# Windowed attention in six layers: each head's scores and values on its own 64 rows of TensorE, and a new split of the PSUM banks

## What is computed

```python
def attn_layer(x, Wqkv, qs, ksc, Wo):          # 16 heads of 64
    q, k, v = jnp.split(x @ Wqkv, 3, -1)
    q = l2norm(q) * qs; k = l2norm(k) * ksc
    q, k = rotary(q), rotary(k)
    out = local_attention(q, k, v)             # windows of 32 queries, 64 keys
    return out @ Wo

def local_attention(q, k, v):                  # this window and the one before it
    sim = jnp.einsum('bhwie,bhwje->bhwij', bq, bk2) * QK_SCALE
    sim = jnp.where(mask, -jnp.finfo(sim.dtype).max, sim)
    attn = jax.nn.softmax(sim, -1)
    return jnp.einsum('bhwij,bhwje->bhwie', attn, bv2)

def ffn_layer(x, ...):                         # layer norm, then a gated MLP
    a, gate = jnp.split(hg, 2, -1)
    return a * jax.nn.gelu(gate, approximate=False) @ W2 + b2
```

## Time and profile before

| what | value |
| --- | --- |
| three runs | 4799.48, 4806.38, 4807.76 us; median 4806.38 |
| profiled execution, own time | 4815.81 us |
| its span, first to last instruction | 4814.0 us |
| TensorE matmul busy, share of the span | 93% |
| VectorE busy | 78% |
| ScalarE busy | 63% |
| GpSimd busy | 37% |
| granted TensorE clock, mean | 0.964 |

### The profile page before, as it was taken

The page is one execution under the profiler, slowest core; times in us unless marked ns, Lnnn a source line. Parts: engine busy times, 40 slices in busy tenths (PEclk is TensorE's granted clock), DMA queues, the critical chain, the costliest instruction groups (busy, mean ns, idle before and its releaser), DMA issues. The chain is left out here.

```text
span 4814.0 us, 118285 instructions
## 1 busy us (share of the span) xinstructions
PE 4463.8 (93%) x45408; PEld 3472.9 (72%) x45408; DVE 3737.9 (78%) x6437; ACT 3030.9 (63%) x4718; POOL 1797.1 (37%) x966
## 2 busy tenths in 40 slices
PE   7999589999999999999999999999999999689999
PEld 2333278787787877778778777787778788468878
DVE  6888588888888888888888888888888888556554
ACT  5777357676766766676667666676766676334333
POOL 0000155554454544555445554455545555000000
PEclk9988799999999999999999999999999999889999
DMA  0000122222322222222222222222222222100000
GB/s 28 5 5 5 46 58 60 54 55 51 84 51 58 58 57 70 58 56 54 70 63 56 54 59 69 58 58 58 51 74 60 58 55 55 61 7 5 9 7 5
DMA packets 132797, 229.65 MB, mean 48 GB/s; under 512 B 29080, under 2 KB 33824, under 8 KB 131104
## 3 DMA queue, kind: packets, MB, share of 16 engines
q1 hardware_dynamic: 132256, 222.28, 17.7%
HBM read 29.23 MB, written 4.19 MB: 7 GB/s over the span
## 5 line engine op out<-in xcount | busy, mean ns | idle before, releaser
L660 POOL TENSOR_TENSOR qk_rotated<-qk_rotated,rotary_sines 128x1024 f32<-128x1024 f32 x384 | 914.9, 2383 | 1407.3 <-DVE rotary_sines L748 1407.2
L671 POOL TENSOR_TENSOR qk_rotated<-qk_rotated,rnorm 128x1024 f32<-128x1024 f32 x384 | 747.0, 1946 | 316.6 <-DVE rnorm L814 309.3
L756 DVE TENSOR_REDUCE qk_sumsq<-qk_squared 128x16 f32<-128x1024 f32 x384 | 467.4, 1217 | 297.5 <-ACT qk_squared L502 297.5
L221 PE MATMUL ps_proj<-qkv_w_hi,x_shifted_hi 128*128 128x512 f32 x1152 | 494.4, 429 | 44.9 <-DVE qkv_w_lo L716 24.0
L509 ACT ACTIVATE q_t<-ps_qk_t 128x512 f32<-128x512 f32 x384 | 229.5, 598 | 461.1 <-PE ps_qk_t L277 461.1
L738 DVE TENSOR_TENSOR qk_rotated<-ps_proj,rotary_scaled 128x1024 f32<-128x1024 f32 x384 | 466.1, 1214 | 4.4 <-ACT qk_squared L502 4.4
L748 DVE TENSOR_TENSOR rotary_sines<-ps_proj,rotary_scaled 128x1024 f32<-128x1024 f32 x384 | 465.6, 1212 | 0.5 <-POOL qk_rotated L660 0.5
L523 ACT ACTIVATE k_t_by_head<-ps_qk_t 64x512 f32<-64x512 f32 x768 | 452.0, 589 | 12.5 <-PE ps_qk_t L286 3.1
L223 PE MATMUL ps_proj<-qkv_w_hi,x_shifted_lo 128*128 128x512 f32 x1152 | 458.7, 398 | 0.0
L222 PE MATMUL ps_proj<-qkv_w_lo,x_shifted_hi 128*128 128x512 f32 x1152 | 457.8, 397 | 0.0
L502 ACT ACTIVATE qk_squared<-ps_proj 128x1024 f32<-128x1024 f32 x384 | 392.2, 1021 | 68.2 <-DVE qk_sumsq L756 50.4
(11 more groups left out here) (248 smaller groups left out, 9847.4 us busy)
## 6 DMA issues: line engine op xcount, KB each, us to landing
v_by_window<-v_tokens SPq DMA_DIRECT2D x1152, 128.0 KB, 2.4
v_by_window<-v_tokens SPq DMA_DIRECT2D x384, 64.0 KB, 2.1
v_by_window<-v_by_window SPq DMA_DIRECT2D x192, 64.0 KB, 2.0
qkv_w_raw<-in_layer_qk_dram SPq DMA_DIRECT2D x7, 1664.0 KB, 7.6
layer_w<-in_layer_w_dram SPq DMA_DIRECT2D x6, 580.5 KB, 3.8
layer_w<-in_layer_w_dram SPq DMA_DIRECT2D x6, 512.0 KB, 3.4
f_x<-in_x_dram SPq DMA_DIRECT2D x8, 256.0 KB, 5.8
x_attn<-f_y SPq DMA_DIRECT2D x8, 256.0 KB, 2.0
```

The source lines that it names most:

```text
L221: mm(out, hi, HI[:, o:o + 512], start=True, stop=False)
L660: tt(u, u, TB[:], ALU.add).then_inc(added, 1)
L671: tt(u, u, r.unsqueeze(3).broadcast_to((P, 2, 8, DH)), ALU.mult).then_inc(scaled, 1)
L756: nc.vector.reduce_sum(SS[:, 16 * i:16 * i + 16], SQ[:].rearrange("p (h e) -> p h e", e=DH), AX).then_inc(sumsq, 1)
```

## The change

Each head gets its own 64 rows. k is kept once (k_t, each head on its own rows, no zeros), and v_by_window loses its zero halves. A score call now has 64 rows, 32 weight columns and 64 moving columns, and is issued for each head: 32 calls in score and 32 in pv, on tiles of 64x32. The two heads of a pair (z) write to two different banks, and each of these banks holds scores in one half and attention output in the other. All four transposes (q, k, output, probabilities) go through one bank, ps_transposed. The mask and the shift become two matmuls of 256 columns each. Because of the shared banks, VectorE now does norm_out before row_max, row_max also waits for pv, and each transpose waits until the previous one has been copied out. On TensorE the shift moves behind the first piece of other work, k_t moves behind the first half of the second piece, and projections and hidden01 are cut in two for that. The k copy on ScalarE becomes one instruction for 128 rows.

```diff
-        KD = sb("k_t_by_head", [P, 2, NC_, KW])
+        KT = sb("k_t", [P, NC_, KW])
-        V2 = sb("v_by_window", [P, NW, 2, NC_, DH])
+        V2 = sb("v_by_window", [P, NW, NC_, DH])
...
-        TP, S, A, X = ps("ps_qk_t"), ps("ps_scores"), ps("ps_attention"), ps("ps_tail")
+        SA, TP, X = ps("ps_scores_attn", 2 * 512), ps("ps_transposed"), ps("ps_tail")
+        S = [SA[:, 512 * z:512 * z + 256] for z in range(2)]
+        A = [SA[:, 512 * z + 256:512 * z + 512] for z in range(2)]
+        S_BY_HEAD = SA[:].rearrange("p (z a c k) -> p a z c k", z=2, a=2, k=DH)[:, 0]
+        A_BY_HEAD = SA[:].rearrange("p (z a c k) -> p a z c k", z=2, a=2, k=DH)[:, 1]
...
-                    sp.dma_start(V2[k + WIN:k + DH, 0, h], VT[0:WIN, 0, h]).then_inc(v2_in, 16)
+                    sp.dma_start(V2[k + WIN:k + DH, 0], VT[0:WIN, 0, h]).then_inc(v2_in, 16)
...
+            def q_t(g, previous):
...
                     pe.wait_ge(scaled, g.n + 1)
-                    after(pe, kt_out, g.n * 2)
+                    after(pe, pt_out, previous.n)
...
+            def k_t(g, previous):
...
                     pe.wait_ge(qt_out, g.n + 1)
+                    after(pe, ot_out, previous.n + 1)
...
-                mm(S[:].rearrange("p (c k) -> p c k", k=P), IDR[:], MASKR[:, g.t:g.t + 1, :].broadcast_to([P, 4, P]), start=True, stop=False,
-                   skip_group_check=True)
+                for z in range(2):
+                    mm(S[z].rearrange("p (c k) -> p c k", k=DH), IDR[:], MASKR[:, g.t:g.t + 1, 0:DH].broadcast_to([P, 4, DH]), start=True, stop=False,
+                       skip_group_check=True)
...
+                pe.sem_inc(score_go, 1)
                 for c in range(4):
-                    for w in range(4):
-                        q, k = g.t * P + WIN * w, base + WIN * w
-                        last = mm(S[WIN * w:WIN * w + WIN, c * P:(c + 1) * P], QT[:, 4 * g.half + c, q:q + WIN],
-                                  KD[:, :, 4 * g.half + c, k:k + 2 * WIN], start=False, stop=True, skip_group_check=True)
+                    for z in range(2):
+                        rows = slice(DH * z, DH * z + DH)
+                        for w in range(4):
+                            q, k = g.t * P + WIN * w, base + WIN * w
+                            last = mm(S[z][WIN * w:WIN * w + WIN, c * DH:(c + 1) * DH], QT[rows, 4 * g.half + c, q:q + WIN],
+                                      KT[rows, 4 * g.half + c, k:k + 2 * WIN], start=False, stop=True, skip_group_check=True)
...
+            def probs_t(g, turned, attended):
...
                     pe.wait_ge(exped, g.n + 1)
-                    after(pe, ot_out, g.n)
+                    if turned.live:
+                        pe.wait_ge(kt_out, turned.n + 1)
+                    elif attended.live:
+                        pe.wait_ge(ot_out, attended.n + 1)
...
+            def pv(g, cleared):
...
                 pe.wait_ge(pt_out, g.n + 1)
+                after(pe, o_norm, g.n)
                 pe.wait_ge(v2_in, g.m.n * V2DMA + (V2TILE0 if g.t == 0 else V2DMA))
+                pe.sem_inc(pv_go, 1)
...
+            def out_t(g, turned, scored):
...
                     pe.wait_ge(o_norm, g.n + 1)
+                    if turned.live:
+                        pe.wait_ge(qt_out, turned.n + 1)
...
                 score(gs[1])
-                pv(ga[1])
-                q_t(gt[1])
-                shift(gs[1])
+                pv(ga[1], gs[1].live)
+                q_t(gt[1], gs[1])
                 q1(n1)
                 mean(e)
-                out_t(ga[1])
-                k_t(gt[1])
+                shift(gs[1])
+                out_t(ga[1], gt[1], gs[1])
...
-                hidden01(h, n1)
-                probs_t(gs[1])
+                hidden0(h, n1)
+                k_t(gt[1], ga[1])
+                hidden1(h)
+                probs_t(gs[1], gt[1], ga[1])
                 variance(e)
 
                 score(gs[2])
-                pv(ga[2])
-                q_t(gt[2])
+                pv(ga[2], gs[2].live)
+                q_t(gt[2], gs[2])
+                hidden2(h, e)
                 shift(gs[2])
-                hidden2(h, e)
-                out_t(ga[2])
-                k_t(gt[2])
+                out_t(ga[2], gt[2], gs[2])
                 k1(n1, h)
+                k_t(gt[2], ga[2])
                 mix(h)
-                probs_t(gs[2])
+                probs_t(gs[2], gt[2], ga[2])
...
-                for h in range(2):
-                    r = slice(DH * h, DH * h + DH)
-                    a(KD[r, h, 4 * g.half:4 * g.half + 4, base:base + P], TP[r, :].rearrange("p (c k) -> p c k", k=P),
-                      ACT.Copy).then_inc(kt_out, 1)
+                a(KT[:, 4 * g.half:4 * g.half + 4, base:base + P], TP[:].rearrange("p (c k) -> p c k", k=P), ACT.Copy).then_inc(kt_out, 1)
...
-            nc.gpsimd.memset(KD[:], 0.0).then_inc(setup, 1)
+            nc.gpsimd.memset(KT[:], 0.0).then_inc(setup, 1)
...
-            def row_max(g):
+            def row_max(g, attended):
 
                 if g.live:
                     dve.wait_ge(scores, g.n + 1)
-                    nc.vector.tensor_reduce(NMX[:], S[:].rearrange("p (a e) -> p a e", e=DH), AX, ALU.max, negate=True).then_inc(nmax, 1)
+                    if attended.live:
+                        dve.wait_ge(pv_mm, attended.n + 1)
+                    nc.vector.tensor_reduce(NMX[:].rearrange("p (z c) -> p z c", z=2), S_BY_HEAD, AX, ALU.max, negate=True).then_inc(nmax, 1)
```

122 lines of the change are left out of this document (69 added, 53 removed).

## The result

The changed kernel takes 5124.56 us (median of 4 runs, 5117.06 to 5129.73) against 4807.07: 1.066 times as long, 95% interval 1.0639 to 1.0681. The forecast was 4930, up to 5060. The direction was right, the size was not: 317 us slower, not 123.

A forecast was written before the change was run, and what follows sets the result against it. The prediction saw a three-engine loop bounding the 36 us turn; +0.4 and +1.1 us gave +1.5 in 84 turns, +126 us, less 3 for halved clears: 4930 us on the median's scale. Its own range was 4870 to 5000, with rivals 4760 to 5060.

The forecast's parts named there:

- Leg C: unchanged: VectorE's stretch from the last sum of squares through row maximum, newton, slots 0 and 1 to the next sines: stays 23.3 us.
- With pv done by then: Slot 3, VectorE: pv is finished when VectorE reaches norm_out and row_max after its sum of squares, so no added wait.
- Score and pv, I take 0.5: TensorE's score and pv: each function falls from about 0.9 to 0.5 us, about 0.85 us less work a slot.
- a fixed price per matmul: Rival on TensorE: each matmul keeps its 0.028 us, 1.8 us a function, about +7.5 a turn, 5520 us; chance 0.05.
- I count nothing for them: Two turns a layer where VectorE also divides the next weights: its added work replaces waits, so zero cost.
- So no engine alone sets the 36 us: Ordinary turn of 36.01 us: bounded by a loop through TensorE, ScalarE and VectorE, not by one engine.
- since the next square waits for the sum before it anyway: Slot 0: v1_first's 1.5 us wait for the sines delays k_t and probs_t, but costs at most 0.1 us.
- Legs A and B: TensorE from slot 1's sines to probs_t, +0.4 us; then mostly ScalarE to VectorE's last sum of squares, +1.1 us.
- at nothing to 0.1 us: TensorE's score_go and pv_go semaphore increments: issued ahead of the array, costed at nothing to 0.1 us.
- TensorE paces after all, faster: Rival: k_t of slot 2 waits below 0.3 us; turn 35.6 us, 4770 us, or 4720 with more gains; chance 0.16.
- the clock: Rival: TensorE's added idling lowers its granted clock, its work grows 8%, +1.3 us a turn more, 5040 us; chance 0.08.
- No concurrency of the row halves: Rival: score and pv stay at 0.9 us on TensorE, +1.1 us a turn more, 5020 us; chance 0.12.

The follow-up runs named there:

- dve_order: The kernel before with only VectorE changed: norm_out before row_max, and row_max waits for pv; 5054 us, ratio 1.0504.
- out_first: The changed kernel with slot 2's attn_out transposed before the shift and copied before ScalarE's third gate; 5095 us, ratio 1.0604.
- one_go: The changed kernel with pv's three waits moved in front of score and the second semaphore step left out; 5351 us, ratio 1.1128.
- half_score: The changed kernel with half of the heads' scores left out, 32 score matmuls in place of 64; 5000 us, ratio 1.0401.

## Why the prediction was right and wrong, point by point

- **"Leg C: unchanged"** is the step that failed first. It grew by 1.0 us, of the 1.1 us by which the turn measured above, 38.6 us, exceeds the forecast of 37.5. "With pv done by then" was wrong in slot 3 (norm_out waits 0.50) and in slot 0 (0.23). dve_order shows the size of what I had costed at nothing: VectorE's order and wait alone are +246 us in the kernel before.
- **"Score and pv, I take 0.5"** was too low. From the start of score to the start of q_t it is 1.55 us; I had 1.0, before 1.88. The eight tiles do overlap, but the saving is 0.33 us a slot, not 0.85. This and leg C belong together: by these numbers, a pv that ended 0.5 us earlier would have ended most of norm_out's two waits. That is an estimate, no run shows it.
- **Not in the forecast at all**: the price of 50,688 more instructions. 105 us of pauses stand in pv. The mean turn is 0.9 us above the one without a pause, where before it was 0.3 above the ordinary one: 95 x 0.6 = 57 us, an estimate of what reached the end. Of the rivals, "a fixed price per matmul" was nearest in kind, but took the price for one per call; here it goes by density.
- **"I count nothing for them"**, of the long turns, failed as well. The 14 turns that took over 38 us before are 40 us longer together, 2.9 us each; the other full turns grew by 3.3.
- **"So no engine alone sets the 36 us"** is the step that led me there. The legs are a true description of a loop. But TensorE was busy 35.26 of 36.01 us, so a new wait there has almost nothing to hide in, and I went through three legs in place of listing TensorE's new waits. I counted k_t's in slot 2, and took v1_first's (forecast 1.5 us, measured 1.01) as harmless "since the next square waits for the sum before it anyway". hidden0's wait for the sines (0.92 us in this turn) and the pauses have no price in the forecast. That TensorE alone sets the turn isn't shown either: VectorE's order and wait alone cost 246 us in the kernel before, and a wait taken away came back in part at another place (out_first: 72 us less before k_t, 30 us of time).
- **Legs A and B** held: 2.5 us for a forecast of 2.3, 11.8 for 11.95; k_t of slot 2 waits 0.79 us for a forecast of 0.9, and ScalarE's saved copy turned into idle time (0.94 us before probs_t_out). VectorE's wait for the last square did not grow; it fell from 1.93 to 1.50 us.
- **The increments "at nothing to 0.1 us"**: the run without the second one, and with pv's waits moved ahead, is 226 us slower (one_go), mostly by longer pauses. What the increment costs or gives by itself is open.
- **The rivals**: k_t of slot 2 waited more than 0.3 us, so "TensorE paces after all, faster" did not happen; the clock stayed at 1.00 in the turns shown, so the 5040 us of "the clock", nearest in size, would have been luck. "No concurrency of the row halves" (5020 us) is wrong in kind, but its direction shows: score to pv is 0.77 us for 0.90 before. The halves do overlap, 10 ns a matmul for 26, but twice as many matmuls use up most of that.
- **The sum**: forecast +1.5 us in 84 turns. Measured: +2.6 in the turn without a pause (the legs) and +0.6 in the mean over it, +3.2 in 95 turns, 304 us; the span of the two profiled executions grew by 301.

## What to carry to other kernels

Before walking through legs, take the engine that is busiest and subtract: with 93% busy, list every wait that a new order puts on that engine, and count each until something shows that it is covered. Two buffers that come to share a bank can cost more than their own wait: here the wait for pv alone was 141 us, and the order of the reader that went with it 105 more. And where many tiny calls replace fewer, leave other work between the blocks; making the stream denser can make it slower.

## What the runs showed of the hardware that was not expected

- Matmuls on eight tiles of 64x32 start (0.86 - 0.224) / 63 = 10 ns apart, with a weight load for each; on four tiles of 128x32 with twice the columns it was (1.08 - 0.276) / 31 = 26 ns. The Trainium skill, page "TensorE: Matmul & The Clock Gate", section "Back-to-back issue gap", gives an issue floor of about 25 ns for few columns; these rows don't agree across tiles: 10 ns is less.
- A block of 64 + 64 such matmuls with its loads uses about as many instructions as a 16 KB packet of the instruction queue holds. In dense blocks TensorE then stood still, 1.94 us in the row shown, in the middle of a group of independent matmuls, with no releaser in the trace: idle before pv's matmuls is 105 us in the changed kernel, 232 when the blocks followed each other, 61 with four transposes between them, 0.7 before the change. Most of these pauses return at the same matmul in each of five layers (65 of 96 in the changed kernel).
- A quarter of the 64-column calls less (half_score) went with half of these pauses in pv: 54 us for 105.
